# Node scores by TensorE, and six sorting chunks in place of five, in a graph attention kernel

## The chip, the cores and the metric

The kernel runs on one core of one Trainium2 chip. The metric is the device time of one execution in microseconds. Five engines work side by side, each on its own instructions in order: PE (TensorE, matmuls; PEld is its weight load), DVE (VectorE), ACT (ScalarE), POOL (GpSimd) and SP (SyncE, which here only issues DMAs). They wait for one another through semaphores.

## What is computed

`x` holds 6250 nodes of 128 features; 100,000 edges have a source node, a destination that plays no part in the result, and 128 features. The reference, cut to what matters:

```python
h = relu(layernorm(x))
edge_h = concatenate([h[src], edge_embed], axis=1)      # 256 wide
edge_m = edge_h @ a.T                                   # a is 128 x 256
edge_e = exp(-leaky_relu(edge_m @ a_2[0], 0.2))
rowsum = segment_sum(edge_e, src)
h_prime = segment_sum(edge_e[:, None] * edge_m, src)
out = x + h_prime / rowsum
```

The score of an edge is linear in both halves, so it splits into a node part (`relu(...) . node_w`, with `node_w = a[:, :128].T @ a_2`, scaled by the node's `rstd`) and an edge part. The sum over the edges of a node needs only `exp` times the raw edge features; the products with `a` are done once per node.

## The kernel before

Nodes stand in 49 windows of 128 (`WINDOWS`), edges in 784 tiles of 128. Eight tiles are a group (98 groups, counted from 0), seven groups a round (14 rounds, 56 tiles each). Rounds are gathered into chunks, `CHUNKS = [2, 4, 4, 3, 1]`. Each chunk is sorted by source window and then summed:

- `count_chunk` (L976, DVE) makes 50 masks, one per window, as wide as the chunk has tiles; `scan_chunk` (L985) runs one prefix sum over 50 times that width, copies its ends (L989), and for chunks after the first multiplies half of it by the masks (L994). PE turns the ends into offsets (`rank_sums`).
- `rank_chunk` (DVE from L1002) works out offsets in some ten small steps, waits for one matmul of PE (`first_tiles`, L785), and makes 50 "picks", each a product over the chunk's tiles; PE adds every pick into one PSUM row with an f32 matmul against the identity (L792 for chunk 0, with five pick buffers; L801 and L804 later, where ACT makes every second pick). An f32 matmul shows in the trace as two passes, each with its own weight load; an f32 transpose as one. The row is cast and packed (L1031 to L1042) into the place of every edge.
- `table_chunk` makes the table by which the summing steps are steered.
- A *feed* (one group): DVE ends the group before and starts the next (L1135, L1116), PE looks node scores up (L850), ACT takes the exponential and scales eight tiles (L652 to L660), and POOL sends them to their sorted places in DRAM with eight indirect DMAs, the *scatters* (L563), 782 in all. There are 14 feed slots: group g + 14 is loaded by SP only when group g has been scattered.
- *Pairs*: the sorted rows of a chunk come back and are summed by PE (L885), eight matmuls a step, seven steps a round, one round more than the chunk has. DVE and ACT make the one-hot operands (L1212, L717), DVE adds the sums (L1183, L1173). A chunk's pairs can begin when all of its groups are scattered. The DRAM rows are zeroed first (`fill`, L390), one fill for each round of pairs.

What runs when on DVE, PE and ACT is written by hand in `PLAN`; each entry is emitted in that order on each engine: `("feed", g, n)` feeds n groups from g; `("pairs", c, r0, r1, g, per)` runs rounds r0 to r1 of chunk c with `per` feeds from g in each. SP has its own order: at the start source numbers, `x`, edge group 0, the first fill, then the place rows of groups 0 to 2, and so on.

The node part before: DVE takes mean and variance (L1083 and on), ACT does 49 ReLUs (L615, one per window), POOL multiplies seven windows at a time by `node_w` (L548), ACT sums each window with an accumulating copy (L619). `nodes` (DVE, L1105) waits for all 49 and splits the scores into three bf16 parts for the look-ups. Later, at `("self",)`, PE transposes each window (L839), ACT copies the result (L640), PE multiplies it by `a`'s node half (L831), and ACT saves the products (L631), in 17 units of three windows.

Of the kernel before, what the change touches and what calls it, by code (L numbers as in the profile page):

```python
# [27 lines left out]
ALU = mybir.AluOpType  # L28
# [9 lines left out]
P = 128  # L38
# [12 lines left out]
RG = 7  # L51
# [6 lines left out]
CHUNKS = [2, 4, 4, 3, 1]  # L58
# [15 lines left out]
FIN_UNITS = -(-WINDOWS // NW)  # L74
ADD_LAG = 2
# [16 lines left out]
    ("count", 0), ("stats",), ("scan", 0), ("rank", 0), ("nodes",), ("feed", 0, 2), ("table", 0), ("feed", 2, 6), ("self",),  # L92
    ("count", 1), ("scan", 1), ("feed", 8, 3), ("rank", 1), ("feed", 11, 3), ("table", 1), ("feed", 14, 7),
    ("pairs", 0, 0, 3, 21, 4), ("count", 2), ("scan", 2), ("feed", 33, 5), ("rank", 2), ("table", 2), ("feed", 38, 13),
    ("pairs", 1, 0, 2, 51, 4), ("count", 3), ("scan", 3), ("feed", 59, 3), ("rank", 3), ("table", 3), ("pairs", 1, 2, 5, 62, 4),
    ("count", 4), ("scan", 4), ("feed", 74, 2), ("rank", 4), ("table", 4), ("feed", 76, 3),
# [82 lines left out]
def gnn_kernel(nc, x, src, edge_attr, a, a_2, out):  # L179
    ctx = ExitStack()  # L180
    with ctx:
# [29 lines left out]
        node_w = sb("node_w", [P, FEAT], F32)  # L211
# [52 lines left out]
        SCORES = 6  # L264
# [11 lines left out]
        def bank(b, lo, n, rows=P):  # L276
# [8 lines left out]
            dve_hot apart_done act_hot step_done rest_cleared first_cleared ranked relu_done terms_done dots_done selfT_done selfT_copied self_scaled pool_added rest_zero acc_done inv_done scaledT_done scaledT_copied  # L285
# [6 lines left out]
         dve_hot, apart_done, act_hot, step_done, rest_cleared, first_cleared, ranked, relu_done, terms_done, dots_done, selfT_done, selfT_copied, self_scaled, pool_added, rest_zero, acc_done, inv_done, scaledT_done, scaledT_copied,  # L292
# [15 lines left out]
        node_terms = back[:, 0:WINDOWS * FEAT].rearrange("p (w f) -> p w f", f=FEAT)  # L308
# [45 lines left out]

        def row_tags(slot):

            return feed_g[:, bass.ds(slot, 1), :].rearrange("p g (u r) -> p (g u) r", r=ROW)

        FILL_AHEAD = 7
# [7 lines left out]
        def _(sp):  # L367
# [60 lines left out]
            for k in range(1, RG):  # L428
                pass_on(0, k, True)
                load(RG + k, RG + k, k)  # L430
                if k % 2 == 1:
                    fill(fills, fill_chunk[fills])
                    fills += 1
# [71 lines left out]
        def _(pool):  # L505
# [84 lines left out]
        def _(act):  # L590
# [13 lines left out]
            act.copy(node_w[:, :], bank(SCORES, 0, P)).then_inc(weights_copied, 1)  # L604
# [5 lines left out]
            def node_relu():  # L610
# [3 lines left out]
                for w in range(WINDOWS):  # L614
                    act.activation(acc[:, w * ROW:w * ROW + FEAT], acc[:, w * ROW:w * ROW + FEAT], ACT.Relu,  # L615
                                   bias=moments[:, w, 0:1]).then_inc(relu_done, 1)
                for w in range(WINDOWS):
# [3 lines left out]
            def windows_of(n):  # L621
# [672 lines left out]
```

## Time and profile before

| | us |
|---|---|
| median of 3 runs | 1156.25 (1155.75 to 1156.82) |
| the profiled execution | 1157.21 |
| its span | 1155.5 |
| DVE, POOL, ACT, PE busy | 834.4, 806.9, 622.5, 611.8 |
| the 782 scatters (POOL L563), busy | 767.5 |
| first and last scatter start | 76.8 and 1085.6 |

The profile is of one execution, and the sum of a prediction is made against its 1157.21 us, of which 1.7 us lie outside the span. Busy shares are averages over a start (preparation of nodes and of chunk 0), a long middle (feeding, scattering, sorting, summing) and an end (the last sums and the products). The granted clock of TensorE (PEclk) stands at 0.50 or 1.00, which are 1.2 and 2.4 GHz.

### The profile page before, as it was taken

How to read it: one execution, taken by the hardware profiler on the slowest of the kernel's cores; microseconds unless marked ns; L12 is line 12 of the kernel's file. 1: busy time of each engine (PE TensorE's matmuls, PEld its weight loads, DVE VectorE, ACT ScalarE, POOL GpSimd, SP SyncE). 2: the span in 40 equal slices, each digit the busy share in tenths (PEclk: the TensorE clock that was granted, in tenths of full speed). 3: DMA queues.
4: the chain of work that ended last, by engine and by line, in shares of the span. 5: the costliest groups of instructions: out<-in, count | busy, mean ns of one | idle time of the engine just before them, and what ended most of it. 6: DMA issues, size and time to landing. Idle time of an engine off the chain costs nothing. (4 is left out here: it accounts for less than half of the span.)

```text
span 1155.5 us, 21963 instructions
## 1 busy us (share of the span) xinstructions
PE 611.8 (53%) x5524; PEld 539.6 (47%) x5525; DVE 834.4 (72%) x3065; ACT 622.5 (54%) x2067; POOL 806.9 (70%) x826
## 2 busy tenths in 40 slices
PE   1144446246762163111655168762767562979997
PEld 0143436235551153111544167652656452778886
DVE  7986976888689957543557969768486543957787
ACT  3926435547562344423545257962376652888775
POOL 2727776777778777777777777777777777777402
PEclk9975758557786576555768578885578786989999
DMA  9999994999873744749887478974797769679744
GB/s 285 359 337 369 384 335 140 317 348 324 303 235 102 251 127 132 261 136 340 262 283 251 131 268 264 314 242 130 234 353 260 239 209 298 193 270 295 250 148 112
DMA packets 203971, 291.55 MB, mean 252 GB/s; under 512 B 19368, under 2 KB 144519, under 8 KB 203751
## 3 DMA queue, kind: packets, MB, share of 16 engines
q1 hardware_dynamic: 160852, 167.63, 45.4%
q10 hardware_dynamic: 18002, 69.95, 17.6%
q0 software_dynamic: 25024, 52.90, 12.9%
q8 instruction: 38, 0.62, 0.2%
q14 instruction: 55, 0.44, 0.1%
HBM read 158.94 MB, written 131.47 MB: 251 GB/s over the span
## 5 line engine op out<-in xcount | busy, mean ns | idle before, releaser
L563 POOL DMA_INDIRECT ordered_rows<-feed,dest x782 | 767.5, 982 | 267.3 <-issue 241.3
L885 PE MATMUL psum<-back,hots 128*128 128x129 f32 x2128 | 335.6, 316 | 36.1 <-DVE hots L1212 25.3
L885 PEld LDWEIGHTS psum<-back,hots 128*128 128x128 f32 x2128 | 300.0, 222 | 76.3 <-issue 74.9
L717 ACT ACTIVATE apart<-lanes,back 128x128 bf16<-128x128 bf16 x504 | 161.3, 389 | 184.9 <-PE psum L885 154.9
L660 ACT ACTIVATE feed<-feed 128x128 f32<-128x128 f32 (+1 forms) x784 | 238.7, 387 | 0.2 <-issue 0.2
L850 PE MATMUL psum<-score_parts,place_hot 128*128 128x50 bf16 x2352 | 99.6, 204 | 244.5 <-DVE place_hot L1116 224.9
L850 PEld LDWEIGHTS psum<-score_parts,place_hot 128*128 128x128 bf16 x2352 | 90.8, 110 | 255.5 <-DVE place_hot L1116 233.8
L1116 DVE TENSOR_SCALAR place_hot<-place_rows,lane 128x1024 bf16<-128x1024 bf16 (+1 forms) x98 | 52.0, 530 | 171.2 <-SPq L412 169.4
L1125 DVE SCALAR_TENSOR_TENSOR junk<-feed,psum 128x128 bf16<-128x128 f32 x784 | 169.8, 279 | 0.0
L652 ACT ACTIVATE feed<-leaky 128x8 f32<-128x8 f32 (+2 forms) x98 | 20.4, 208 | 245.0 <-DVE leaky L1148 245.0
L1212 DVE TENSOR_TENSOR hots<-psum,back 128x512 f32<-128x512 f32 (+1 forms) x133 | 94.4, 710 | 4.0 <-DMA back<-ordered_rows 4.0
L1183 DVE TENSOR_TENSOR acc<-acc,psum 128x387 f32 (+1 forms) x119 | 66.0, 555 | 31.6 <-PE psum L885 17.9
L1024 DVE SCALAR_TENSOR_TENSOR picked<-sorting,shift 128x112 f32<-128x112 bf16 (+3 forms) x150 | 52.4, 374 | 43.4 <-PE psum L801 42.0
L721 ACT ACTIVATE hots<-apart 128x512 f32<-128x512 bf16 (+1 forms) x133 | 80.8, 607 | 4.2
L872 PE MATMUL psum<-zeros 1*128 1x387 bf16 x105 | 39.8, 379 | 64.5 <-DVE acc L1183 61.4
L680 ACT ACTIVATE picked<-sorting,shift 128x224 f32<-128x224 bf16 (+2 forms) x100 | 43.0, 434 | 55.8 <-PE psum L804 42.3
L985 DVE TENSOR_TENSOR_SCAN sorting<-sorting,psum 128x11200 bf16<-128x11200 bf16 (+2 forms) x4 | 70.6, 17653 | 0.1
L1143 DVE TENSOR_REDUCE zed<-chosen 128x8 f32<-128x408 f32 x98 | 56.6, 578 | 9.3 <-DVE chosen L1135 7.1
L1125 DVE DVE_READ_ACCUMULATOR junk<-feed,psum 128x1 f32 x784 | 62.7, 80 | 0.0
L777 PE MATMUL psum<-ends,below 128*128 128x50 bf16 x5 | 1.1, 222 | 115.2 <-DVE ends L989 115.2
L1135 DVE TENSOR_TENSOR chosen<-psum,window_hot 128x400 f32<-128x400 f32 x98 | 55.4, 565 | 6.6 <-PE psum L850 6.3
L1119 DVE TENSOR_TENSOR window_hot<-psum,bucket 128x400 bf16<-128x400 f32 x98 | 55.2, 563 | 0.0
(161 smaller groups left out, 734.1 us busy)
## 6 DMA issues: line engine op xcount, KB each, us to landing
ordered_rows<-empty SPq DMA_DIRECT2D x19, 3696.0 KB, 18.2
back<-ordered_rows ACTq DMA_DIRECT2D x123, 528.0 KB
feed<-in_edge_attr SPq DMA_DIRECT2D x97, 512.0 KB, 6.2
place_rows<-places SPq DMA_DIRECT2D x98, 256.0 KB, 5.8
ordered_rows<-feed,dest POOLq DMA_INDIRECT x782
back<-ordered_rows SPq DMA_DIRECT2D x10, 528.0 KB
self_part<-acc ACTq DMA_DIRECT2D x1, 3234.0 KB, 15.0
acc<-in_x SPq DMA_DIRECT2D x4, 768.0 KB, 8.5
```

Source lines behind the costliest of these rows:

```text
L563: pool.indirect_dma_start(out=ordered, out_offset=bass.IndirectOffsetOnAxis(ap=dest[:, n:n + 1], axis=0), in_=feed[:, n * ROW:(n + 1) * RO ...
L660: last = act.activation(emb, emb, ACT.Copy, scale=tags[:, u, PROB:PROB + 1])
L717: act.activation(apart[:, v * P:(v + 1) * P], lanes[:, :], ACT.Abs, bias=tags[:, u, PLACE:PLACE + 1], scale=-1.0).then_inc(apart_done, 1)
L721: act.activation(hots[:, u0 + n:u0 + GT, :].rearrange("p u n -> p (u n)"), apart[:, 0:mine * P], ACT.Relu, bias=1.0, scale=-1.0).then_inc( ...
L850: last = pe.matmul(bank(SCORES, u * BUCKETS, BUCKETS), place_hot[:, u * P:(u + 1) * P], score_parts[:, part, :], start=part == 0, stop=par ...
L885: last = pe.matmul(psum[:, bass.ds(outs[u], FEAT + 1)], hots[:, hot_buffer(k) * GT + u, :], back[:, n:n + FEAT + 1], start=False, stop=u = ...
L985: done(dve.tensor_tensor_scan(count[:, 0:flat], hot[:, 0:flat], none, 0.0, ALU.add, ALU.max))
L1125: dve.scalar_tensor_tensor(out=junk[:, u, :], in0=feed[:, bass.ds((slot * GT + u) * ROW, FEAT)], scalar=1.0, in1=bank(CONSTS, EDGE_W, FEAT ...
L1135: dve.tensor_tensor(chosen[:, :, 0:BUCKETS], bank(SCORES, 0, GT * BUCKETS).rearrange("p (t w) -> p t w", w=BUCKETS), window_hot[:, :, :], ...
L1143: dve.tensor_reduce(zed[:, :], chosen[:, :, :], axis=AX_X, op=ALU.add).then_inc(zed_done, 1)
L1183: dve.tensor_tensor(sums[:, 0], sums[:, 0], new[:, 0], ALU.add).then_inc(acc_done, 1)
L1212: dve.tensor_tensor(hots[:, u0:u0 + n, :], bank(CONSTS, LANES, P).rearrange("p (a n) -> p a n", a=1).to_broadcast(shape), tags[:, 0:n, PLA ...
```

## The change

Two things are changed together.

**Node scores.** POOL's multiplications and ACT's 49 accumulating copies are gone. ACT still does the ReLUs, three windows at a time; PE transposes each window (`node_unit`), ACT copies the three turned blocks into `reluT` (all 49 stay there), and PE multiplies each turned block, as the stationary operand, by `node_w`, now one column, into one PSUM column (`dots`). There are 17 such units on PE: eight before `rank_sums(0)`, four between `rank_sums(0)` and `first_tiles(0)`, and five each behind one of the first five batches of five picks. `nodes` reads the scores from PSUM. The entry `("self",)` only multiplies the stored `reluT` blocks and saves.

**Chunks.** `CHUNKS` is `[1, 2, 3, 4, 3, 1]`: chunk 0 has one round. `PLAN` is written anew: four groups are fed before the second chunk is counted (eight before), the first pairs begin at group 21 as before, and the pairs of the last four-round chunk start at group 81 (79 before), with group 97 alone in their fifth round. There are 20 fills and 20 rounds of pairs in place of 19.

```diff
-CHUNKS = [2, 4, 4, 3, 1]
+CHUNKS = [1, 2, 3, 4, 3, 1]
...
+UNITS_FIRST = 8
...
 PLAN = [
-    ("count", 0), ("stats",), ("scan", 0), ("rank", 0), ("nodes",), ("feed", 0, 2), ("table", 0), ("feed", 2, 6), ("self",),
...
-    ("pairs", 2, 0, 4, 79, 4), ("pairs", 2, 4, 5, 95, 3),
-    ("pairs", 3, 0, 4, 98, 0), ("pairs", 4, 0, 2, 98, 0),
+    ("count", 0), ("stats",), ("scan", 0), ("rank", 0), ("nodes",), ("feed", 0, 2), ("table", 0), ("feed", 2, 2), ("self",),
+    ("count", 1), ("scan", 1), ("feed", 4, 2), ("rank", 1), ("feed", 6, 2), ("table", 1), ("feed", 8, 6),
...
+    ("pairs", 3, 0, 4, 81, 4), ("pairs", 3, 4, 5, 97, 1),
+    ("pairs", 4, 0, 4, 98, 0), ("pairs", 5, 0, 2, 98, 0),
 ]
...
-        node_w = sb("node_w", [P, FEAT], F32)
+        node_w = sb("node_w", [P, 1], F32)
...
-            pool.wait_ge(weights_copied, 4)
-            for i in range(WINDOWS // RG):
-                at = slice(RG * i, RG * i + RG)
-                pool.wait_ge(relu_done, RG * (i + 1))
-                pool.tensor_tensor(node_terms[:, at, :], acc_w[:, at, 0:FEAT],
-                                   node_w[:, :].rearrange("p (a f) -> p a f", a=1).to_broadcast([P, RG, FEAT]),
-                                   ALU.mult).then_inc(terms_done, 1)
...
-                for w in range(WINDOWS):
-                    act.wait_ge(terms_done, w // RG + 1)
-                    act.activation(node_terms[:, w, :], node_terms[:, w, :], ACT.Copy, accum_out=score[:, w:w + 1]).then_inc(dots_done, 1)
...
+                def turned(n):
+
+                    at = windows_of(n)
+                    act.wait_ge(selfT_done, n + 1)
+                    act.copy(reluT[:, at.start * P:at.stop * P], bank(n % 2, 0, (at.stop - at.start) * P)).then_inc(selfT_copied, 1)
+
+                for n in range(FIN_UNITS):
+                    for w in range(WINDOWS)[windows_of(n)]:
+                        act.activation(acc[:, w * ROW:w * ROW + FEAT], acc[:, w * ROW:w * ROW + FEAT], ACT.Relu,
+                                       bias=moments[:, w, 0:1]).then_inc(relu_done, 1)
+                    if n > 0:
+                        turned(n - 1)
+                turned(FIN_UNITS - 1)
...
+            def node_unit(n):
+
+                def dots(n):
+
+                    pe.wait_ge(selfT_copied, n + 1)
+                    for w in range(WINDOWS)[windows_of(n)]:
+                        last = pe.matmul(bank(NODE_DOTS, w, 1), reluT[:, w * P:(w + 1) * P], node_w[:, :], start=True, stop=True)
+                    last.then_inc(dots_done, 1)
+
+                if n >= 2:
+                    pe.wait_ge(selfT_copied, n - 1)
+                for w in range(WINDOWS)[windows_of(n)]:
+                    pe.wait_ge(relu_done, w + 1)
+                    last = pe.transpose(bank(n % 2, (w - NW * n) * P, P), acc_w[:, w, 0:FEAT], ident[:, :])
+                last.then_inc(selfT_done, 1)
+                if n > 0:
+                    dots(n - 1)
+                if n == FIN_UNITS - 1:
+                    dots(n)
...
-                if what == "scan":
+                if what == "stats":
+                    pe.wait_ge(weights_copied, 4)
+                    for n in range(UNITS_FIRST):
+                        node_unit(n)
+                elif what == "scan":
                     rank_sums(at[0])
+                    if at[0] == 0:
+                        for n in range(UNITS_FIRST, 12):
+                            node_unit(n)
                 elif what == "rank":
                     first_tiles(at[0])
                     if at[0] == 0:
                         for i in range(BUCKETS // BB):
                             pick_sums(i)
+                            if 12 + i < FIN_UNITS:
+                                node_unit(12 + i)
```

How instructions stand now is shown at two places. The first is PE from its last preparing matmul to the first look-ups. Before, in order: the setup matmuls, the three of `rank_sums` (L777 to L779), `first_tiles` (L785), the 50 picks of 112 columns (L792), the look-ups (L850).

```order
L771 MATMUL psum<-hots 128x128
L777 MATMUL psum<-ends,below 128x50
L778 MATMUL psum<-ends,above 128x50
L779 MATMUL psum<-ends,ones_bf 128x51
L785 MATMUL psum<-ident,tiles_before 50x1
L792 MATMUL psum<-picked,ident 128x112 x50
L850 MATMUL psum<-score_parts,place_hot 128x50 x72
```

In the changed kernel the same stretch begins with transposes (L834) and dots (L827); here from the eighth unit on.

```order
L834 MATMUL psum<-ident,acc 128x128 x3
L827 MATMUL psum<-node_w,back 128x1 x3
L775 MATMUL psum<-ends,below 128x50
L776 MATMUL psum<-ends,above 128x50
L777 MATMUL psum<-ends,ones_bf 128x51
...
L783 MATMUL psum<-ident,tiles_before 50x1
L790 MATMUL psum<-picked,ident 128x56 x5
L834 MATMUL psum<-ident,acc 128x128 x3
L827 MATMUL psum<-node_w,back 128x1 x3
L790 MATMUL psum<-picked,ident 128x56 x5
```

So `rank_sums` stands behind eight units, `first_tiles` behind twelve, and after each of the first five batches of picks PE does one unit more.

The second place is DVE after the start of the last group (98th, started by L1116 before, L1131 now, in a feed that ends at L1125 and L1140). Before, that start lies inside the fifth round of the four-round chunk's pairs, two steps after the feed ahead of it:

```order
L1212 TENSOR_TENSOR hots<-psum,back 128x512
L1135 TENSOR_TENSOR chosen<-psum,window_hot 128x8x50
L1143 TENSOR_REDUCE zed<-chosen 128x8
L1148 SCALAR_TENSOR_TENSOR leaky<-zed 128x8
L1116 TENSOR_SCALAR place_hot<-place_rows,lane 128x1024
L1119 TENSOR_TENSOR window_hot<-psum,bucket 128x400
L1125 SCALAR_TENSOR_TENSOR junk,chosen<-feed,psum 128x128 x8
```

Now it is the end of the fourth round, and the whole fifth round follows it as steps alone (L1227 in each):

```order
L1131 TENSOR_SCALAR place_hot<-place_rows,lane 128x1024
L1134 TENSOR_TENSOR window_hot<-psum,bucket 128x400
L1140 SCALAR_TENSOR_TENSOR junk,chosen<-feed,psum 128x128 x8
L338 TENSOR_LOAD table
L1190 COMPARE_AND_BRANCH
...
L1227 TENSOR_TENSOR hots<-psum,back 128x512
L338 TENSOR_LOAD table
```

What moved: seven steps stand between the start of the last group and its end, where three stood before.

## Rows read from the trace of the kernel before

**Rows 1.** Page, part 5: group, out<-in xcount | busy, mean ns | idle before.

```profile
L563 POOL DMA_INDIRECT ordered_rows<-feed,dest x782 | 767.5, 982 | 267.3 <-issue 241.3
```

**Rows 2.** Timeline of POOL: start us, us, what [idle before <-releaser].

```profile
27.45 24.25 POOL L548 TENSOR_TENSOR back<-acc,node_w 128x896 f32<-128x896 f32 x7 [19.66 <-ACT acc L615]
76.82 1.15 POOL L563 DMA_INDIRECT ordered_rows<-feed,dest  x1 [25.12 <-ACT feed L660]
...
120.22 3.96 POOL L563 DMA_INDIRECT ordered_rows<-feed,dest  x1 [0.30 <-issue]
...
198.23 1.14 POOL L563 DMA_INDIRECT ordered_rows<-feed,dest  x1 [4.47 <-issue]
...
1085.61 0.96 POOL L563 DMA_INDIRECT ordered_rows<-feed,dest  x1 [0.31 <-issue]
```

**Rows 3.** Timeline of DVE, the start: chunk 0, and two feeds later.

```profile
8.76 4.98 DVE L976 TENSOR_SCALAR sorting<-bucket 128x112 bf16<-128x112 bf16 x50
...
25.66 11.76 DVE L985 TENSOR_TENSOR_SCAN sorting<-sorting 128x5600 bf16<-128x5600 bf16 x1
...
43.69 0.20 DVE L1002 COPY rows_before<-psum 128x51 f32<-128x51 f32 x1
...
52.93 14.12 DVE L1024 SCALAR_TENSOR_TENSOR picked<-sorting,shift 128x112 f32<-128x112 bf16 x50
67.62 0.28 DVE L1031 CAST picked<-psum 128x112 int32<-128x112 f32 x1 [0.57 <-PE psum L792]
...
83.47 0.57 DVE L1135 TENSOR_TENSOR chosen<-psum,window_hot 128x400 f32<-128x400 f32 x1 [0.30 <-DVE table L1073]
...
87.98 0.57 DVE L1135 TENSOR_TENSOR chosen<-psum,window_hot 128x400 f32<-128x400 f32 x1
```

**Rows 4.** DVE: rank of chunk 1 (timeline); the one-round chunk by form.

```profile
162.41 0.20 DVE L1002 COPY rows_before<-psum 128x51 f32<-128x51 f32 x1
...
165.06 1.18 DVE L1024 SCALAR_TENSOR_TENSOR picked<-sorting,shift 128x224 f32<-128x224 bf16 x3
...
L985 DVE TENSOR_TENSOR_SCAN sorting<-sorting,psum 128x2800 bf16<-128x2800 bf16 x1 | 6.0, 5985 | 0.0
...
L976 DVE TENSOR_SCALAR sorting<-bucket 128x56 bf16<-128x56 bf16 x50 | 4.3, 200 | 0.0
```

**Rows 5.** SyncE's waits, 0 to 100 us: total, times, longest.

```profile
SPq L412 <- DMA place_rows<-places: 9.1, 1, 9.1
```

**Rows 6.** Windows of PE alone: stretch, length, busy (passes), PEclk, DMA share, GB/s.

```profile
54.00:58.00 4.00, 4.00 (x21) 1.00 1.17 313
58.00:62.00 4.00, 4.00 (x36) 1.00 1.19 295
...
806.00:810.00 4.00, 4.00 (x20) 0.50 0.40 90
...
116.00:120.00 4.00, 4.00 (x37) 0.98 1.06 391
```

**Rows 7.** Timeline of PE: picks of the one-round chunk, transposes.

```profile
805.78 0.63 PE L801 MATMUL psum<-picked,ident 128*128 128x56 f32 x2
806.20 0.63 PE L804 MATMUL psum<-picked,ident 128*128 128x56 f32 x2
...
104.80 1.52 PE L839 MATMUL psum<-ident,acc 128*128 128x128 f32 x6
```

**Rows 8.** Timeline of ACT: the ReLUs, one copy of three turned blocks.

```profile
25.16 14.40 ACT L615 ACTIVATE acc<-acc,moments 128x128 f32<-128x128 f32 x49
...
121.47 0.48 ACT L640 COPY hots<-psum 128x384 f32<-128x384 f32 x1
```

**Rows 9.** Timeline of DVE near the end.

```profile
968.37 0.68 DVE L1116 TENSOR_SCALAR place_hot<-place_rows,lane 128x1024 bf16<-128x1024 bf16 x1 [20.39 <-SPq L412]
...
1023.88 0.69 DVE L1212 TENSOR_TENSOR hots<-psum,back 128x512 f32<-128x512 f32 x1 [2.39 <-DMA back<-ordered_rows]
...
1091.61 0.96 DVE L1212 TENSOR_TENSOR hots<-psum,back 128x768 f32<-128x768 f32 x1 [1.26 <-DMA back<-ordered_rows]
```

More of the change, by code:

```diff
@@ L91 @@
 PLAN = [
-    ("count", 0), ("stats",), ("scan", 0), ("rank", 0), ("nodes",), ("feed", 0, 2), ("table", 0), ("feed", 2, 6), ("self",),
[L93 to L96, printed above, removed]
-    ("pairs", 2, 0, 4, 79, 4), ("pairs", 2, 4, 5, 95, 3),
-    ("pairs", 3, 0, 4, 98, 0), ("pairs", 4, 0, 2, 98, 0),
+    ("count", 0), ("stats",), ("scan", 0), ("rank", 0), ("nodes",), ("feed", 0, 2), ("table", 0), ("feed", 2, 2), ("self",),
+    ("count", 1), ("scan", 1), ("feed", 4, 2), ("rank", 1), ("feed", 6, 2), ("table", 1), ("feed", 8, 6),
+    ("count", 2), ("scan", 2), ("feed", 14, 3), ("rank", 2), ("table", 2), ("feed", 17, 4),
+    ("pairs", 0, 0, 2, 21, 4), ("feed", 29, 6),
+    ("count", 3), ("scan", 3), ("feed", 35, 3), ("rank", 3), ("table", 3), ("feed", 38, 3),
+    ("pairs", 1, 0, 3, 41, 4), ("feed", 53, 3),
+    ("count", 4), ("scan", 4), ("feed", 56, 2), ("rank", 4), ("table", 4),
+    ("pairs", 2, 0, 2, 58, 4), ("count", 5), ("scan", 5), ("feed", 66, 2), ("rank", 5), ("table", 5),
+    ("pairs", 2, 2, 4, 68, 4), ("feed", 76, 5),
+    ("pairs", 3, 0, 4, 81, 4), ("pairs", 3, 4, 5, 97, 1),
+    ("pairs", 4, 0, 4, 98, 0), ("pairs", 5, 0, 2, 98, 0),
 ]
@@ L430, in _ @@
                 load(RG + k, RG + k, k)
-                if k % 2 == 1:
+                if k % 2 == 1 or k == RG - 1:
                     fill(fills, fill_chunk[fills])
@@ L603, in _ @@
             act.wait_ge(weights_step, 2)
-            act.copy(node_w[:, :], bank(SCORES, 0, P)).then_inc(weights_copied, 1)
+            act.copy(node_w[:, :], bank(SCORES, 0, 1)).then_inc(weights_copied, 1)
             act.wait_ge(pool_set, 25)
@@ L632, in save @@
                        .then_inc(self_copied, 1)
[L634 removed]
+                act.wait_ge(dots_done, FIN_UNITS)
                 for n in range(FIN_UNITS):
[L636 to L644 removed]
+                    save(n)
                 act.wait_ge(self_copied, FIN_UNITS)
@@ L770, in _ @@
             pe.matmul(bank(CONSTS, EDGE_W, FEAT), a2_wide, a_sb[:, FEAT:2 * FEAT], start=True, stop=True)
-            pe.matmul(bank(SCORES, 0, P), a2_wide, a_sb[:, 0:FEAT], start=True, stop=True)\
+            pe.matmul(bank(SCORES, 0, 1), a_sb[:, 0:FEAT], a2_wide[:, 0:1], start=True, stop=True)\
               .then_inc(weights_step, 1)
@@ L821, in table_sums @@
                           start=True, stop=True).then_inc(pairs_done, 1)
+            def node_unit(n):
[14 more added lines that the diff above has]
+                    dots(n)
             def self_products():
-                def product(n):
-                    pe.wait_ge(selfT_copied, n + 1)
+                pe.wait_ge(selfT_copied, FIN_UNITS)
+                for n in range(FIN_UNITS):
                     if n >= 2:
                         pe.wait_ge(self_copied, n - 1)
-                    for k in range(min(WINDOWS, NW * n + NW) - NW * n):
-                        last = pe.matmul(bank(2 + n % 2, k * P, P), last_T[:, n % 2, k, :], A1w[:, :], start=True, stop=True)
+                    for w in range(WINDOWS)[windows_of(n)]:
+                        last = pe.matmul(bank(2 + n % 2, (w - NW * n) * P, P), reluT[:, w * P:(w + 1) * P], A1w[:, :], start=True, stop=True)
                     last.then_inc(self_done, 1)
-                pe.wait_ge(relu_done, WINDOWS)
-                for n in range(FIN_UNITS):
-                    if n >= 2:
-                        pe.wait_ge(selfT_copied, n - 1)
-                    for k, w in enumerate(range(NW * n, min(WINDOWS, NW * n + NW))):
-                        last = pe.transpose(bank(n % 2, k * P, P), acc_w[:, w, 0:FEAT], ident[:, :])
-                    last.then_inc(selfT_done, 1)
-                    if n > 0:
-                        product(n - 1)
-                product(FIN_UNITS - 1)
             def look_up(g):
@@ L1101, in nodes @@
             def nodes():
-                dve.wait_ge(dots_done, WINDOWS)
+                dve.wait_ge(dots_done, FIN_UNITS)
                 full, rest = score[:, :], score_rest[:, 0:WINDOWS]
-                done(dve.tensor_tensor(full, full, rstd[:, :], ALU.mult))
+                done(dve.tensor_tensor(full, bank(NODE_DOTS, 0, WINDOWS), rstd[:, :], ALU.mult))
                 done(dve.tensor_copy(score_parts[:, 0, 0:WINDOWS], full))
```

27 lines of the change are left out of this document (7 added, 20 removed).

## The prediction

> **What bounds the kernel now.** I read the page's costliest groups first: POOL's 782 scatters are busy 767.5 us [rows 1]. POOL's own timeline then shows that they stand nearly wall to wall: the first starts at 76.8, the last at 1085.6 [rows 2], 1008.8 us apart. The most frequent distance between two is 1.264 us (0.96 of work, 0.30 of issue), 781 of them make 987.2, and 21.6 us are left for irregular gaps: scatters stretched while DVE runs long bf16 instructions (3.96 us at 120.2), and one late feed (4.5 us idle at 198.2) [rows 2]. So the time is three stretches in a row: what comes ahead of the first scatter, the scatters, and the 71.6 us from the last one's start to 1157.2, which wait for that scatter. DVE and PE matter where they delay the first scatter, let POOL run dry, or are late at the end.
>
> Ahead of the first scatter the timeline of DVE shows one engine without a pause: masks, statistics, scan, offsets, 50 picks, ending at 67.6, and 9.2 us from there to the first scatter (score parts, look-up, exponential, scaling) [rows 2, 3]. PE does almost nothing there until the picks.
>
> **The start, DVE's side.** The masks of 56 tiles take 4.3 us for 5.0, the scan 6.0 for 11.8 [rows 3, 4]: 6.4 saved. While POOL multiplied, from 27.5 to 51.7 [rows 2], DVE's small steps were long: from L1002 to the first pick 9.2 us in chunk 0, 2.65 in chunk 1 for the same steps [rows 3, 4], so 6.6 saved. Against that, group 0's place rows land only at 32.7, after a wait of SP of 9.1 us [rows 5], so DVE waits for them from 31.3. By DVE alone the picks could begin at 32.7 + 2.6 (starting group 0) + 2.65 = 38.0 in place of 52.9.
>
> **The start, PE's side.** This is the term that decides. All node work now stands on PE, in order, ahead of and between what DVE waits for. Its price per pass is read from the picks of the one-round chunk: two f32 matmuls of 56 columns start 0.42 apart, 0.213 a pass, 20 passes in 4 us [rows 6, 7]. Chunk 0's picks of 112 columns ran at the same pace at first (21 in 4 us), then at 36 in 4 us [rows 6]: the pace of a slow pass does not depend on the width up to 112 columns; the weight load sets it. Six transposes take 1.52 us, the last of them 0.46, so again 0.21 each [rows 7]. The dots have one column, but a weight load as all others. I take 0.213 for every pass.
>
> The passes: 49 transposes, 49 dots of two passes, 50 picks of two passes, 247 in all, 52.6 us. In order: ReLUs start at 24.5 (25.2 less the 0.6 of the masks) and take 0.29 each [rows 8], so PE has two units of transposes and the first dots behind it at 28.0. A unit is nine passes, 1.92 us, more than ACT's three ReLUs and a copy (0.88 + 0.48 [rows 8] = 1.36), so PE sets the pace: eight units end at 28.0 + 6 x 1.92 = 39.5, rank_sums at 39.7, twelve at 47.4, first_tiles at 47.9. DVE picks from 48.1, 4.8 earlier than before. But now PE needs 50 x 0.427 = 21.3 us for the picks and 9.6 for five units between them, and is done at 79.4; L1031 starts at 79.6, where it started at 67.6 [rows 3]. The 9.2 us behind it stay (casts half as wide, -0.4; a look-up at the lower clock, +0.4). **The first scatter moves from 76.8 to 88.8: +12.0.** Gains of DVE end in waits for PE.
>
> Why slow passes throughout? The granted clock reads 1.00 up to 71.9 us, but the passes say otherwise: 21 in 4 us at 54 to 58, 36 from 58 on, the same two paces that stand beside 0.50 and 0.98 later [rows 6]. So the reading of the first 70 us is not to be trusted, and PE starts at 1.2 GHz. It rose after four us of 112-column picks, and in the self products after six. It did not rise in the one-round chunk: the same picks at the same pace, PE busy all the time, 56 columns, 0.50 from 804 to 828 without a break (its first full window is in rows 6). In the changed kernel chunk 0's picks are exactly these, and the units ahead of them have six one-column passes to three transposes. That is nearest to the stretch that stayed at 0.50.
>
> **The middle.** Only POOL running dry counts. Taking T as the first scatter, DVE reaches the count of chunk 1 at T + 15 with four groups fed. Then come masks (5.0, as in rows 3), the scan (11.8), its product (about 1.6), two groups (3.9 each; up to 4.5 [rows 3]), 2.65 of offsets, and the picks of 112 columns shared with ACT, about 18 with the clock rising as it did for 112 columns: group 6 is fed at T + 69, and its turn on POOL is at T + 61 plus some 3 of stretched scatters. That is about 5 us of idling, where group 11 had 4.5 [rows 2]. Five counts in place of four may stretch one more scatter (0 to 5 us, 2 taken). Later every cover is 8 us or more by the same count: POOL needs 10.1 us a group, DVE 4.5. I take **+3**, bounds -2 and +8. The 20th fill and the seven added steps lie beside scatters.
>
> **The end.** At 948 to 968 DVE waits 20.4 us for SP, which waits for a slot [rows 9]; that moment is tied to POOL and stays. Behind it stood 14 steps and seven feeds; now 18 steps and seven feeds, since the fifth round comes later by two groups. One step fits into the following wait for SP, three do not: at 2.4 us a step (28 steps from 1023.9 to 1091.6, less the wait [rows 9]) 7.2 us. The next chunk's pairs then start with their rows already there: the bubble of 3.9 us at 1020 to 1024 (2.4 of it DVE's wait) is filled, leaving +3.3, and 1.3 of slack stood ahead of the last chunk [rows 9]. **+2**, bounds 0 and +8.
>
> **The sum**: 1157.2 + 12.0 + 3 + 2 = 1174.2 for a profiled execution; this one was 1.0 above the median, so **1173**.
>
> **The rivals.**
> 1. *PE at the full clock from the first units.* Passes of 0.111 (36 in 4 us [rows 6]) make a unit 1.0, less than ACT's 1.36. Twelve ReLU units end at 24.5 + 12 x 1.36 + 0.9 = 41.7, picks begin near 42.7, and 50 x 0.222 + 5.0 end at 58.8: -8.8. With +3 and +2 and -1.0: **1152**, faster than before. For it: the clock did rise in the first picks and in the self products. Against it: the one-round chunk. It decides if the clock is up before about 40 us. Chance 0.15; this is also what the page's Part 1 would give.
> 2. *The clock rises in between*, at the interleaved picks or a little before: 1158 to 1166. Chance 0.12.
> 3. *The second chunk starves POOL.* If its picks of 112 columns stay slow (0.85 a pair for 0.5, 25 pairs) group 6 comes 9 us later still: **1182**. For it: it alternates with ACT as the one-round chunk did. Against: these are twice as wide. Chance 0.11.
> 4. *The forecast*, 1167 to 1181 with the bounds. Chance 0.62.
>
> **How the numbers follow.** A measurement of this kernel can tell 0.2%, 2.3 us, from no change. Faster: most of rival 1, some of which ends within 2.3 us: 0.12. Same: the rest of it and the low edge of rival 2: 0.08. Slower: 0.80. The range takes in the forecast with its bounds, rivals 2 and 3, and none of rival 1: 1156 to 1186.
>
> **What would show it.** The first scatter's start (88.8 by me, 68 by rival 1); passes of PE between 26 and 78 (about 19 or 36 in 4 us, whatever the granted clock reads); waits of DVE for PE ahead of the first offset step (L1002) and in the picks; POOL's largest idle time near its 48th scatter; the wait of DVE ahead of the last chunk, gone. What would make it wrong: dots that run beside each other's loads, a clock that counts loads, or a feed that starves late.

## The result, and the profile after

The changed kernel takes **1179.6 us** (1178.2 to 1181.8, five runs), the kernel before beside it 1156.3 (1155.4 to 1158.5): 1.0201 times as long, 95% interval 1.0187 to 1.0216. It is slower, as forecast, and 6.6 us slower than the 1173 of the forecast.

The page of the changed kernel, for [rows 1]: the span and POOL's scatters (L566 now; the columns are those of the costliest groups).

```profile
span 1177.5 us, 22970 instructions
...
L566 POOL DMA_INDIRECT ordered_rows<-feed,dest x782 | 763.9, 977 | 330.1 <-issue 244.0
```

The scatters are busy 3.6 us less than before. The idle time ahead of them grew by 62.8 us, but 54.4 of that stand ahead of the first one (79.52 below, 25.12 before [rows 2]), since POOL's own multiplications are gone and the first scatter is late; so idle time does not tell the cost, and the stretches below do. POOL's timeline (start us, us, engine line op, in brackets the idle time before it and what ended it), answering [rows 2]:

```profile
87.30 1.13 POOL L566 DMA_INDIRECT ordered_rows<-feed,dest  x1 [79.52 <-ACT feed L658]
...
153.75 0.96 POOL L566 DMA_INDIRECT ordered_rows<-feed,dest  x1 [5.09 <-ACT feed L658]
...
274.87 1.04 POOL L566 DMA_INDIRECT ordered_rows<-feed,dest  x1 [7.93 <-issue]
...
1100.80 0.96 POOL L566 DMA_INDIRECT ordered_rows<-feed,dest  x1 [0.30 <-issue]
```

The first scatter starts at 87.3 (76.8 before), the last at 1100.8 (1085.6). So the three stretches are:

| us | first scatter | first to last scatter | last scatter to the end | span |
|---|---|---|---|---|
| before | 76.8 | 1008.8 | 69.9 | 1155.5 |
| after | 87.3 | 1013.5 | 76.7 | 1177.5 |
| difference | +10.5 | +4.7 | +6.8 | +22.0 |
| forecast | +12 | +3 | +2 | |

**The start** is what PE is. Windows of PE's busy time in the changed kernel (us, PE busy with the number of passes, granted clock, DMA share, GB/s), against [rows 6]:

```profile
30.00:34.00 4.00, 4.00 (x21) 1.00 0.98 291
...
54.00:58.00 4.00, 4.00 (x21) 1.00 0.99 274
...
70.00:74.00 4.00, 4.00 (x21) 1.00 0.00 0
```

PE works from 25 to 78 with one pause of 0.6 us, and never gets past 23 passes in 4 us. The column of the granted clock says 1.00 in all of them, as it did before the first clock record in the old trace (here the first record begins at 106.5); the pace of the passes is the one that stands beside 0.50 elsewhere [rows 6]. What DVE waited for between 26 and 78 (us in total, times, longest):

```profile
DVE picked L1039 <- PE psum L790: 11.9, 19, 2.0
DVE first_tile L1031 <- PE psum L783: 5.6, 1, 5.6
DVE rows_before L1017 <- PE psum L777: 4.7, 1, 4.7
DVE picked L1046 <- PE psum L790: 1.9, 1, 1.9
```

DVE was ready for its offsets at 34.5 and got them at 39.2, got the first tiles at 46.8, and saw the last pick summed at 78.0: 24 us of waiting for PE in all, where it had waited 1.1 before (26 to 68).

**The middle** lost 4.8 us at the 49th scatter (group 6) and 7.6 us at the 137th (group 17): the two rows with 5.09 and 7.93 above, less the usual 0.30. In return group 11's 4.2 us of before are gone, and the scatters are busy 3.6 us less, mostly since they are stretched less: 12.4 - 4.2 - 3.6 is 4.6, close to the 4.7 of the table.

**The end.** DVE's timeline at SP's long wait and behind it, answering [rows 9]:

```profile
983.51 0.49 DVE L1131 TENSOR_SCALAR place_hot<-place_rows,lane 128x1024 bf16<-128x1024 bf16 x1 [21.67 <-SPq L423]
...
1046.67 0.57 DVE L1219 COPY psum<-psum 128x387 f32 x1 [0.20 <-DVE acc L1198]
...
1054.25 0.56 DVE L1198 TENSOR_TENSOR acc<-acc,psum  x1 [4.35 <-PE psum L891]
```

The wait ends 117.3 us ahead of the last scatter, as before (117.2): that moment keeps its distance from POOL's last scatter. From there to the last chunk but one (the copy at 1046.67, before at 1020.93) it is 63.2 us, where it was 52.6; from that copy to the first step of the last chunk 67.8, where it was 70.7; from there to the end of the span 63.0, where it was 63.9.

### The profile page after: what moved, and what is told of

Its sections match the earlier page's. It is cut to its first block and busy times, and to the rows that moved or that the text cites. A ratio compares the mean times of both kernels' runs of the same rounds, so it can differ in the third digit from the quotient of the medians.

```text
span 1177.5 us, 22970 instructions
## 1 busy us (share of the span) xinstructions
PE 667.6 (57%) x5872; PEld 595.2 (51%) x5873; DVE 870.2 (74%) x3208; ACT 630.1 (54%) x2029; POOL 778.9 (66%) x819
## 5 line engine op out<-in xcount | busy, mean ns | idle before, releaser
L566 POOL DMA_INDIRECT ordered_rows<-feed,dest x782 | 763.9, 977 | 330.1 <-issue 244.0
L891 PE MATMUL psum<-back,hots 128*128 128x129 f32 x2240 | 350.5, 316 | 34.5 <-DVE hots L1227 21.3
L891 PEld LDWEIGHTS psum<-back,hots 128*128 128x128 f32 x2240 | 313.8, 221 | 75.1 <-issue 73.5
L715 ACT ACTIVATE apart<-lanes,back 128x128 bf16<-128x128 bf16 x532 | 170.2, 389 | 170.2 <-PE psum L891 144.9
L1140 DVE SCALAR_TENSOR_TENSOR junk<-feed,psum 128x128 bf16<-128x128 f32 x784 | 170.0, 281 | 0.0
L1131 DVE TENSOR_SCALAR place_hot<-place_rows,lane 128x1024 bf16<-128x1024 bf16 (+1 forms) x98 | 48.7, 497 | 122.3 <-SPq L423 120.7
L1039 DVE SCALAR_TENSOR_TENSOR picked<-sorting,shift 128x56 f32<-128x56 bf16 (+3 forms) x175 | 59.3, 346 | 59.7 <-PE psum L799 41.8
L1227 DVE TENSOR_TENSOR hots<-psum,back 128x512 f32<-128x512 f32 (+1 forms) x140 | 99.3, 709 | 0.0
L1198 DVE TENSOR_TENSOR acc<-acc,psum 128x387 f32 (+1 forms) x126 | 70.0, 555 | 36.3 <-PE psum L891 24.4
L719 ACT ACTIVATE hots<-apart 128x512 f32<-128x512 bf16 (+1 forms) x140 | 85.2, 608 | 4.4
L678 ACT ACTIVATE picked<-sorting,shift 128x168 f32<-128x168 bf16 (+3 forms) x125 | 51.5, 415 | 54.8 <-PE psum L802 38.1
L878 PE MATMUL psum<-zeros 1*128 1x387 bf16 x112 | 42.3, 377 | 66.5 <-DVE acc L1198 63.2
L1000 DVE TENSOR_TENSOR_SCAN sorting<-sorting,psum 128x8400 bf16<-128x8400 bf16 (+3 forms) x5 | 76.6, 15320 | 0.2
L1140 DVE DVE_READ_ACCUMULATOR junk<-feed,psum 128x1 f32 x784 | 64.2, 82 | 0.0
```

Of the source, the lines that this page charges most:

```text
L566: pool.indirect_dma_start(out=ordered, out_offset=bass.IndirectOffsetOnAxis(ap=dest[:, n:n + 1], axis=0), in_=feed[:, n * ROW:(n + 1) * RO ...
L715: act.activation(apart[:, v * P:(v + 1) * P], lanes[:, :], ACT.Abs, bias=tags[:, u, PLACE:PLACE + 1], scale=-1.0).then_inc(apart_done, 1)
L719: act.activation(hots[:, u0 + n:u0 + GT, :].rearrange("p u n -> p (u n)"), apart[:, 0:mine * P], ACT.Relu, bias=1.0, scale=-1.0).then_inc( ...
L891: last = pe.matmul(psum[:, bass.ds(outs[u], FEAT + 1)], hots[:, hot_buffer(k) * GT + u, :], back[:, n:n + FEAT + 1], start=False, stop=u = ...
L1000: done(dve.tensor_tensor_scan(count[:, 0:flat], hot[:, 0:flat], none, 0.0, ALU.add, ALU.max))
L1039: dve.scalar_tensor_tensor(out=picked[:, k * tiles:(k + 1) * tiles], in0=count[:, at], scalar=shift[:, b:b + 1], in1=hot[:, at], op0=ALU.a ...
```

## Experiments

Each ratio is against runs of the kernel before on the same chip. These had medians of 1153.9 to 1158.9 us, so an expectation in us is compared by the ratio to 1156.3. The stretches are from one profiled execution each.

| kernel | ratio to before (95%) | first scatter | first to last | end | span |
|---|---|---|---|---|---|
| after | 1.020 (1.019 to 1.022) | 87.3 | 1013.5 | 76.7 | 1177.5 |
| scores_only | 1.008 (1.005 to 1.011) | 85.6 | 1009.4 | 68.8 | 1163.9 |
| chunks_only | 1.011 (1.009 to 1.014) | 77.7 | 1012.9 | 73.5 | 1164.1 |
| wide_dots | 1.001 (1.000 to 1.003) | 66.7 | 1010.5 | 74.2 | 1151.4 |
| few_wide | one run, 1172.8 us | 83.1 | 1015.3 | 72.4 | 1170.8 |
| early_feeds | 1.016 (1.012 to 1.019) | 87.3 | 1006.9 | 72.0 | 1166.2 |
| late_fills | 1.012 (1.007 to 1.016) | 87.1 | 1006.2 | 74.3 | 1167.6 |
| tail | 1.013 (1.009 to 1.016) | 87.3 | 1016.0 | 68.6 | 1171.9 |
| wide_plan | 0.989 (0.986 to 0.993) | 67.4 | 1007.2 | 70.8 | 1145.3 |
| wide_all | **0.988 (0.985 to 0.990)** | 66.5 | 1001.4 | 68.6 | 1136.5 |
| wide_old_chunks | 1.001 (0.999 to 1.002) | 69.5 | 1014.3 | 68.7 | 1152.5 |

### The two halves alone

scores_only: node_unit and the rest of the score path as in the change, with the old table of chunks.

```diff
-CHUNKS = [1, 2, 3, 4, 3, 1]
+CHUNKS = [2, 4, 4, 3, 1]
-PLAN = [ ... of the changed kernel
+PLAN = [ ... of the kernel before
```

> One half of the change alone: node scores on TensorE as in the changed kernel, but the old five chunks and their order of work. My account: the middle and the end stay as before, and the start pays for PE's slow passes. The first picks begin near 47.6; the 25 picks (of 112 columns here) between the units run at half pace to about 67, the other 25 speed up after some 4 us as before, and are done near 75; first scatter near 85.5 instead of 76.8: 1165 us (1161 to 1169). Rival 1: the wide picks between the units already lift the clock: picks done by 68, first scatter 77 to 79, 1156 to 1159. Rival 2: the node scores are the whole loss and the chunks nothing: 1179.

Measured 1.008: +9 us, first scatter at 85.6, middle and end those of before. The wide picks between the units did not speed up: 20 or 21 passes in 4 us up to 70, and only when the units were through did the picks speed up (28 in the next 4 us; the first clock record of this trace, at 1.00, begins at 72.3).

```profile
66.00:70.00 4.00, 4.00 (x21) 1.00 1.04 410
70.00:74.00 4.00, 4.00 (x28) 1.00 1.03 416
```

Rivals 1 and 2 of this run are out.

chunks_only: the mirror image, the old kernel with the new CHUNKS, PLAN and fills.

> The other half alone: six chunks and their order of work, node scores on POOL and ACT as before (node_w lies in a free part of hots, since the wider table needs its room). My account: the first scatter is early, at 70 to 75 instead of 76.8 (masks and scan 6.4 shorter, the picks bound by PE at 0.43 each), the middle loses 5 us and the end 7 us against before, as in the changed kernel: 1164 us (1160 to 1169). Both halves then lose about 8 each, and together more than the sum, because the start's gain of the one-round chunk vanishes in waits for PE. Rival: the chunks cost nothing or gain, and the node scores cost everything: 1150 to 1157. Rival: late feeds grow when the first scatter comes earlier: over 1170.

Measured 1.011: +13 us. The middle loses 4.1 us where 5 were expected, the end 3.6 where 7 were, and the first scatter came at 77.7, not at 70 to 75. DVE's timeline says why:

```profile
37.62 1.48 DVE L1008 TENSOR_SCALAR window_tiles_i<-window_tiles_i 128x50 int32<-128x50 int32 x1
39.13 2.01 DVE L1010 TENSOR_SCALAR window_tiles<-window_tiles_i 128x50 f32<-128x50 int32 x1
41.18 2.07 DVE L1011 TENSOR_TENSOR_SCAN tiles_to<-window_tiles 128x50 f32<-128x50 f32 x1
43.28 1.96 DVE L1012 TENSOR_TENSOR tiles_before<-tiles_to,window_tiles 128x50 f32<-128x50 f32 x1
```

In the changed kernel, where POOL does not multiply, each of these takes 0.19 to 0.26 us. Here POOL multiplies until 45.17, and the next small step of DVE, at 45.28, takes 0.21 again; two steps that read PSUM, at 37.14 and 37.37, keep to 0.2 even beside POOL. Then come PE's picks, of 56 columns here and of 112 in the kernel before:

```profile
46.74 21.58 PE L795 MATMUL psum<-picked,ident 128*128 128x56 f32 x100 [0.62 <-DVE picked L1027]
```

```profile
53.32 14.26 PE L792 MATMUL psum<-picked,ident 128*128 128x112 f32 x100 [0.68 <-DVE picked L1024]
```

The narrow ones stay at 20 or 21 passes in 4 us from 50 to 66, so they take 7.3 us longer. The one-round chunk alone brings nothing to the start: masks and scan of 6 us less are paid back by slow picks. Both halves lose, 9 and 13 us, and together they lose 23, about the sum; that they would lose more than the sum was not borne out.

### Is it the clock?

wide_dots: every dot gets 112 equal columns. The passes, the weight loads and the result (column w of bank 4) stay; the work per pass grows 112-fold.

```diff
-        node_w = sb("node_w", [P, 1], F32)
+        node_w = sb("node_w", [P, 112], F32)
-            pe.matmul(bank(SCORES, 0, 1), a_sb[:, 0:FEAT], a2_wide[:, 0:1], start=True, stop=True)\
+            pe.matmul(bank(SCORES, 0, 112), a_sb[:, 0:FEAT], a2_wide[:, 0:112], start=True, stop=True)\
-                        last = pe.matmul(bank(NODE_DOTS, w, 1), ...
+                        last = pe.matmul(bank(NODE_DOTS, w, 112), ...
```

> The changed kernel with each node dot of 112 equal columns instead of one (the same 98 passes and weight loads, 112 times the columns; the extra columns are overwritten or not read). If the slow clock is what makes the start late, and streams of wide float32 matmuls lift it as the old picks of 112 columns did, the pace between 30 and 46 goes from 21 to about 36 passes in 4 us, the picks start near 43 and are done near 60, first scatter 68 to 72: 1162 us (1159 to 1168). If the pace is a price of the weight loads and of their number that no wider matmul can change: first scatter 87 to 88, 1180. If wider dots lift the clock and the 56-column picks lose it again: about 1170 to 1174.

Measured 1.001: **1.8% faster than the change for 112 times the columns**, and the first scatter at 66.7, earlier than any theory had it. Its PE windows:

```profile
26.00:30.00 4.00, 4.00 (x22) 1.00 1.00 283
30.00:34.00 4.00, 4.00 (x36) 1.00 1.03 323
...
42.00:46.00 4.00, 4.00 (x39) 1.00 1.07 330
```

From 30 on PE does 35 to 39 passes in 4 us, but for the window from 38, in which it waits for the first pick (26); the clock records say 1.00 from 29.4 to 60.2. The picks of 56 columns that follow stay fast to their end at 57.3; they are the instructions that ran at half pace in the changed kernel. This settles the term of the start: the passes' price was the clock's, and the clock followed what the dots gave the engine to do. It was in the forecast as rival 1 in its effect, but not in its cause: it needs other dots. The time, 1.001 of 1156.3 or 1158 us, is a little under the 1159 to 1168 expected: the start gives back 20.6 us, and middle and end came 5.5 us shorter in this profile, which nothing in the edit explains.

few_wide: only the first three units are wide.

> The changed kernel with dots of 112 columns in the first three units only (9 of 49 dots, 18 passes, until about 30 us), all later dots of one column. It asks whether the clock, once up, is held by one-column dots, transposes and 56-column picks. If it is held: first scatter near 67, 1156 to 1158 us. If one-column dots lose it: passes go back to 21 in 4 us within some microseconds and the first scatter is at 80 to 87, 1170 to 1180. I give the first 0.4.

```profile
30.00:34.00 4.00, 4.00 (x32) 1.00 1.00 299
34.00:38.00 4.00, 3.94 (x34) 1.00 1.02 386
38.00:42.00 4.00, 4.00 (x24) 0.56 1.03 416
42.00:46.00 4.00, 3.38 (x18) 0.50 1.05 341
```

The clock rose behind three wide units (record from 31.6), and fell at 38.4 in the one-column units, with PE busy 7.94 of the 8 us from 34 to 42. The units came 1.1 to 1.3 us apart there, at ACT's pace, so PE had short waits that its busy share does not show; but in wide_dots they came 1.25 apart in the same stretch, and there the clock held. In few_wide it then stayed at 0.50, through units and 56-column picks, to the last pick at 73.8. First scatter at 83.1: the second theory, which I had given 0.6. It is one run. In this trace, as in those with wide dots, the records start early enough for the granted clock to agree with the pace of the passes.

The Trainium skill (TensorE: Matmul & The Clock Gate, Part 1) puts the throttle's release down to sustained matmul activity. With the wide dots this case's trace agrees; in the changed kernel PE was busy for 53 us with one pause of 0.6, at the slow pace throughout, so here being busy was not enough.

### The middle

early_feeds: groups 6, 17 and 18 are fed ahead of the picks that had delayed them.

```diff
-    ("count", 1), ("scan", 1), ("feed", 4, 2), ("rank", 1), ("feed", 6, 2), ("table", 1), ("feed", 8, 6),
-    ("count", 2), ("scan", 2), ("feed", 14, 3), ("rank", 2), ("table", 2), ("feed", 17, 4),
+    ("count", 1), ("scan", 1), ("feed", 4, 3), ("rank", 1), ("feed", 7, 1), ("table", 1), ("feed", 8, 6),
+    ("count", 2), ("scan", 2), ("feed", 14, 5), ("rank", 2), ("table", 2), ("feed", 19, 2),
```

> The changed kernel with two edits in its order of work: three groups instead of two are fed ahead of the second chunk's picks (group 6 too), and five instead of three ahead of the third chunk's (groups 17 and 18 too). My account: POOL's idle times of 4.8 us at 149 and 7.6 us at 267 are late feeds of groups 6 and 17 and nothing else; both vanish: 1167.5 us (1166 to 1171 if groups 7 or 19 come a little late instead). Rival: POOL's pace there is set by SP's loads, which wait for POOL's slots themselves, so the idle time only moves: 1175 to 1180.

Both idle times vanished, but 4.5 us came back at group 14, whose last tile had been ready 3.3 us ahead of its scatter in the changed kernel, and 1.9 at group 21:

```profile
236.55 1.06 POOL L566 DMA_INDIRECT ordered_rows<-feed,dest  x1 [4.77 <-issue]
```

The middle gained 6.6 us, not 12.4, and the time (1.016, or 1174 us) lies between the two theories. So neither held alone, and the question became what keeps group 14 late. DVE's waits from 70 to 285 in the changed kernel point to it:

```profile
DVE place_hot L1131 <- SPq L423: 15.3, 2, 10.9
```

Both waits stand just ahead of the third chunk's masks. SP issues these rows between fills of 3.7 MB each: six fills from 120 to 200 us, where the kernel before has three. And SP's issuing of the rows is itself held up, for 9.65 us ahead of the second wait:

```profile
184.17 9.65 SPq L386 DMA_DIRECT2D place_rows<-places  x1
...
199.81 0.60 DVE L1131 TENSOR_SCALAR place_hot<-place_rows,lane 128x1024 bf16<-128x1024 bf16 x1 [10.88 <-SPq L423]
...
202.48 6.28 DVE L991 TENSOR_SCALAR sorting<-bucket 128x168 bf16<-128x168 bf16 x50
```

The DMA share is 1.02 between 180 and 200, and 0.31 between 260 and 280 (changed kernel, POOL's windows):

```profile
180.00:200.00 20.00, 15.13 (x16) 0.50 1.02 359
260.00:280.00 20.00, 9.33 (x10) 0.59 0.31 79
```

late_fills: four fills are issued later. They stood at 159, 177, 194 and 198 us in the changed kernel and stand at 182, 191, 221 and 258 now.

```diff
-                if k % 2 == 0 and fills < FILL_AHEAD + 2:
+                if k == 0:
                     fill(fills, fill_chunk[fills])
...
-            def later_round(r, c):
+            def later_round(r, c, more=()):
-                fill(r + FILL_AHEAD, c)
+                if not more:
+                    fill(r + FILL_AHEAD, c)
                 for k in range(RG):
+                    if k in more:
+                        fill(more[k], fill_chunk[more[k]])
...
+            later_round(2, None, {1: FILL_AHEAD - 1, 2: FILL_AHEAD, 4: FILL_AHEAD + 1, 6: FILL_AHEAD + 2})
```

> The changed kernel with three of the fills (3.7 MB each, written by SP's queue) moved from 155 to 200 us, where the DMA engines are full, to 230 to 300, where they were busy 0.15 to 0.4 of the time; a fourth moves a little. My account of the middle now: DVE's waits for place rows of 4.4 us at 176 and 10.9 us at 189 are waits for DMA bandwidth, they delay the third chunk's count, and so group 17. Without those fills they shrink to under 5 in all, group 17 is fed 10 us earlier and POOL's 7.6 us there vanish; group 6's 4.8 us stay: 1172 us (1170 to 1174). Rival: the place rows wait for POOL's slots, not for bandwidth: no change, 1178 to 1181. Rival: the moved fills delay the read-back or the place rows behind them later: slower than 1181.

Measured 1.012, middle 7.3 us shorter than after, group 17 in time. Both waits ahead of the third chunk are gone, SP's issues of place rows take 0.35 us from 163 to 182 and 0.68 at 185, and the masks start 15.4 us earlier:

```profile
185.06 0.68 SPq L386 DMA_DIRECT2D place_rows<-places  x1
...
187.10 6.40 DVE L995 TENSOR_SCALAR sorting<-bucket 128x168 bf16<-128x168 bf16 x50
```

One new wait of 7.7 us stands at 278, behind a moved fill that held SP for 14.3 us; it made no group late:

```profile
263.50 14.27 SPq L401 DMA_DIRECT2D ordered_rows<-empty  x1
...
277.97 0.49 DVE L1135 TENSOR_SCALAR place_hot<-place_rows,lane 128x1024 bf16<-128x1024 bf16 x1 [7.66 <-SPq L423]
```

So it is shown that the fills, which nobody needed yet, delayed the rows that DVE needed next. Whether they did it by filling the DMA engines or by standing ahead in SP's own queue is not separated: the DMA share from 180 to 200 is still 1.01 in late_fills, without a wait, which speaks against full engines alone. The page's median time to landing does not bear on it, though it reads 9.6 us in the changed kernel and 5.2 in late_fills: tail, with the changed kernel's fills and with 15.1 us of the same waits, has 4.9.

### The end

tail: the steps of the last four-round chunk stand two groups earlier, as in the old order.

```diff
-    ("pairs", 2, 2, 4, 68, 4), ("feed", 76, 5),
-    ("pairs", 3, 0, 4, 81, 4), ("pairs", 3, 4, 5, 97, 1),
+    ("pairs", 2, 2, 4, 68, 4), ("feed", 76, 3),
+    ("pairs", 3, 0, 4, 79, 4), ("pairs", 3, 4, 5, 95, 3),
```

> The changed kernel with the order of work before the end as in the old one: three groups instead of five are fed ahead of the last pass over four rounds, so its steps stand two groups earlier. Behind SP's long wait near 962 to 983 then stand 14 steps and seven feeds instead of 18 and seven. My account: the end shortens by what four steps of 2.4 to 2.7 us cost beyond the wait that one of them fills, less the wait for data that returns ahead of the last chunk but one: 1180 - 5 = 1175 us (1173 to 1177). Rival: the end is set by when the last rows are scattered and come back, and the steps fit in anyway: 1179 to 1181.

1.013 against 1.020, which is 1171 us where 1173 to 1177 were expected, and the end 68.6 us long. The stretch from first to last scatter is 2.5 us longer in this profile, 1.2 of it at groups 6 and 17, ahead of the edit. One profile would prove little, since the end of the same order varies: 76.7, 73.5, 74.2, 72.4, 72.0 and 74.3 in the six profiles with the change's end. But the three with tail's order have 68.6, 70.8 and 68.6, and the three with the old chunks 69.9, 68.8 and 68.7. So the order with four steps more behind the wait costs about 5 us on average and 6.8 in the profile that I read, and the old order alone takes them back.

### Together, and what the chunks are worth

> The changed kernel with the wide dots of wide_dots, the earlier feeds of early_feeds and the end of tail together. Start as wide_dots (first scatter 66.7, 20.6 earlier), middle as early_feeds (-6.6), end -3 to -5: against the 1180 of the changed kernel 1180 - 20.6 - 6.6 - 4 = 1149, against the kernel before 0.992 to 0.998. If the parts hinder each other (an earlier start lets POOL run dry in other places): 1153 to 1157.

> Wide dots, earlier feeds, the moved fills and the old end together. Start as wide_dots (first scatter near 67). Middle: group 6 fed in time (early feeds), groups 14 and 17 in time (moved fills), so 5 us of idling less than in wide_plan: first to last scatter 1001 to 1003 instead of 1007.2. End 69 to 71. Span 1138 to 1141, 6 us under wide_plan, against the kernel before 0.983 to 0.987. If the idling of group 14 has another cause than the fills: as wide_plan, 0.989.

wide_plan measured 0.989, faster than the 0.992 to 0.998 expected, with groups 14 and 21 late by 4.5 and 1.8 us. wide_all measured 0.988, where 0.983 to 0.987 were expected. By their profiled spans wide_all is 8.8 us shorter, by the ratios the two cannot be told apart. **wide_all beats the kernel before by 1.2% (1140.5 us)** and the changed one by 3.2%. Its middle, 1001.4 us, has no late feed left but group 7's, 0.9 us; the rest beyond the usual distance is mostly stretched scatters.

wide_old_chunks is scores_only with the wide dots:

> The old five chunks, their order of work, and the node scores on TensorE with dots of 112 columns: it asks what the six chunks are worth once PE runs at the full clock. My account: twelve units end near 41, DVE is free from 42 (the two-round scan ends at 37.4), picks done near 62, first scatter at 72 to 73; middle and end as before: 1155 - 4 = 1151 us, 0.995 to 0.998. The one-round chunk would then be worth 5 to 6 us at the start and cost 4 to 8 in the middle and at the end as long as its order of work is not mended. Rival: the first scatter comes at 67 here too (PE is the bound in both): 0.992.

The first scatter came at 69.5, 7.3 us earlier than before, and the time did not move (1.001). POOL's timeline shows where most of the gain went:

```profile
184.90 0.96 POOL L562 DMA_INDIRECT ordered_rows<-feed,dest  x1 [0.30 <-issue]
196.26 1.14 POOL L562 DMA_INDIRECT ordered_rows<-feed,dest  x1 [10.40 <-issue]
```

Group 11, late by 4.2 us before [rows 2], is now late by 10.1: an earlier start only lets POOL reach the same late feed sooner. Both my theory and its rival had left the middle alone, and were wrong there. Against wide_all, whose smaller chunks have a mended order of work, its span is 16.0 us longer: 3.0 at the start, 12.9 in the middle. But 10.1 of these are group 11, and the old chunks with that group fed earlier were not run. So with the wide dots the one-round chunk is worth 3 us at the start, and what the six chunks are worth in all stays open.

## Why the prediction was right or wrong

**The start: right in mechanism, 1.5 us too long.** PE's half pace from the first unit to the last pick was the deciding term, and wide_dots shows it by taking it away. The sizes: a unit took 1.82 us, not 1.92 (a pass 0.202, not 0.213), so eight units ended at 39.0 (forecast 39.5), twelve at 46.4 (47.4), the picks at 77.9 (79.4). The step from there to the first scatter was 9.3 (9.2). Reading the passes and not the granted clock was what made this term come out; by the clock column rival 1 would have been the forecast. One sum is off by 0.4: 48.1 + 21.3 + 9.6 is 79.0, not 79.4. And "the weight load sets it" was not tested by itself: at the full clock a pass with its load takes 0.11, for 112 columns too.

**The middle: +3 forecast, +4.7 measured, near it by luck.** Group 6 was late by 4.8 us where the forecast had 5, and group 11's 4.2 went away. Even the 5 is a difference of two terms that were each over 2 us too long: POOL was ready for the group at T + 61.7 (forecast T + 64) and got it at T + 66.5 (T + 69); and the steps listed for T + 69 add up to T + 62, the casts and the feed's own way to POOL, some 8 us, not being in the list. The step "later every cover is 8 us or more" failed: group 17 was late by 7.6. It counted POOL's 10.1 us a group against DVE's 4.5, as if DVE could always feed ahead, and took the fills for something that lies beside scatters. In fact six fills stood between 120 and 200 us, DVE stood 15.3 us for place rows behind them, and the third chunk's masks started that much late; late_fills shows this cause. The kernel before had 7.6 us of the same wait ahead of its second chunk's masks, which no term of the forecast priced. The miss was covered by another: the scatters were busy 3.6 us less, where 2 more had been taken for stretched ones.

**The end: +2 forecast, +6.8 measured in this profile, about +5 on average.** That SP's wait is tied to POOL, and that four more steps stand behind it with one of them in the next wait, was right. Two terms were mis-sized. The way from the wait to the last chunk but one grew by 10.6 us, not 7.2: the three steps account for 6.8 at PE's pace of 2.25 (DVE waits for PE between them), and the rest stands beside a lower clock, without an experiment that would make it the cause. PE's windows of the changed kernel, behind the wait,

```profile
1002.00:1012.00 10.00, 8.09 (x87) 0.84 0.76 238
1012.00:1022.00 10.00, 10.00 (x77) 0.71 0.60 171
```

and before, in the same place, full speed with some 105 passes:

```profile
987.00:997.00 10.00, 9.48 (x109) 1.00 0.82 256
```

In the other five profiles of this order the same way grew by 6.1 to 8.6 us, 7.0 on average, which is the forecast's 7.2; so this part of the miss belongs to one profile. The step that failed in all six is the one by which the bubble of 3.9 us is filled. Its wait for data went, but DVE waits for PE at nearly the same place, 4.35 us here and 3.6 to 4.35 in the others; PE in turn waits there 2.9 us for an operand of ACT, which has the last two feeds to do first. With the 1.3 of slack the forecast gave back 5.2 us from the last chunk but one on; this profile gave back 2.9 up to the last chunk, the slack included, and 0.9 behind it.

**The rivals.** Rival 1 and 2 did not occur. Rival 3's condition, slow picks of 112 columns in the second chunk, did not either (36 or 37 passes in 4 us from 136 on, and 15.3 us for the picks where 18 were taken); its price came all the same, from the third chunk. The time lies in the range, as far from the forecast as from its upper end. The start was 1.5 us too long, middle and end were short by 1.7 and 4.8, for reasons that I had not priced: fills ahead of the place rows, and a bubble that only changed its cause. That the sum comes as near as 5 us to the profiled execution is in part luck.

## What to carry to other kernels

Before moving small work to TensorE, ask what it does to the engine's pace: with 49 one-column products among transposes and narrow picks PE stayed at half pace for 53 us, and with the same products made 112 times as wide the stretch was over 20 us shorter. Read the pace from passes per window, not from a clock column ahead of its first record. And when the start of a pipeline is shortened, look for the next late feed at once: its gain can be handed back there, 5.9 of 7.3 us at group 11, unless the order of work and the background transfers are moved with it.

## What the hardware showed that I had not expected

- A clock that is up is lost without a pause of PE in the profile: in few_wide it fell to 0.50 at 38.4 while PE was busy 4.00 of 4.00 us (3.94 in the four ahead), with one-column products and transposes. In wide_dots 56-column picks ran at the full clock from 51.6 to their end at 57.3; whether they would have held it longer is not shown, since few_wide too had kept it for over 6 us behind its last wide dot.
- Chunk 0's picks differ in width between two kernels in which PE stood idle ahead of them: with 112 columns they rose from 21 to 36 passes in 4 us [rows 6]; with 56 they stayed at 20 or 21 for 20 us (chunks_only).
- Small steps of DVE that keep to SBUF took 1.5 to 2.1 us while POOL multiplied and 0.2 otherwise; those that read PSUM took 0.2 beside it as well (chunks_only).
- SP's issuing instruction for one transfer of 256 KB took 0.35 us, or up to 12.1 among fills (changed kernel, at 211).
